# A third bank for the experts' first layer, one SSD block inside the last expert pass, and new instruction lists in a two-layer adaLN kernel

## Reference

```python
h = layernorm(x) * (1 + ca) + sa
x = x + ga * gated_delta_attention(h)      # q, k, v through silu, depthwise conv, silu; scan over 256 tokens of
                                           # S = a S - a b (S k) k' + b v k'; o = q S; then @ Wo.T
h = layernorm(x) * (1 + cb) + sb
x = x + gb * mixture(h)                    # router, top 2 of 8 experts; every expert is 128 -> 512 (silu) -> 128
h = layernorm(x) * (1 + ca2) + sa2
x = x + ga2 * ssd(h)                       # in-projection, causal conv, chunks of 64 tokens: cumsum, exp, two
                                           # first-order scans, state across chunks, normalisation, out-projection
h = layernorm(x) * (1 + cb2) + sb2
x = x + gb2 * ffn(h)                       # 128 -> 512, butterflies folded into the two matrices, gelu, 512 -> 128
```

## Time and profile before

| what | us |
| --- | --- |
| median of 3 runs | 489.74 |
| the runs | 491.87, 489.74, 486.61 |
| the profiled execution | 488.66 |
| its span in the trace | 486.8 |
| TensorE busy | 429.1 (88%) |
| ScalarE busy | 362.7 (74%) |
| VectorE busy | 346.9 (71%) |
| GpSimd busy | 162.7 (33%) |

### The profile page before, as it was taken

One profiled execution on the slowest core, in us unless ns is written; L12 is line 12 of the kernel. 1 busy time (PEld: TensorE's weight loads), 2 busy tenths in 40 slices (PEclk: granted clock), 3 DMA queues, 4 the chain that ended last, 5 costly groups with the idle time before them and its releaser, 6 DMA issues. The chain is left out here.

```text
span 486.8 us, 7163 instructions
## 1 busy us (share of the span) xinstructions
PE 429.1 (88%) x2164; PEld 312.5 (64%) x2164; DVE 346.9 (71%) x897; ACT 362.7 (74%) x629; POOL 162.7 (33%) x231
## 2 busy tenths in 40 slices
PE   4796987869897899999999999999999878999666
PEld 2675845548684776567667666767677556698434
DVE  3565998759899874999999899998325582222872
ACT  4889779587875759699669885869988889555324
POOL 1143840872359751267840272071100002000010
PEclk9789999799999799999999999999999999999899
DMA  7849892036600338000303811000001000000001
GB/s 199 288 127 267 286 309 80 0 85 173 159 2 0 88 99 213 19 0 1 87 1 85 208 39 23 1 1 0 2 0 24 0 1 1 22 1 1 0 1 23
DMA packets 34630, 35.49 MB, mean 73 GB/s; under 512 B 12824, under 2 KB 30752, under 8 KB 34336
## 3 DMA queue, kind: packets, MB, share of 16 engines
q1 hardware_dynamic: 34016, 30.57, 23.8%
q10 hardware_dynamic: 576, 4.46, 2.6%
HBM read 13.78 MB, written 1.05 MB: 30 GB/s over the span
## 5 line engine op out<-in xcount | busy, mean ns | idle before, releaser
L877 PEld LDWEIGHTS psS<-we2s,hid 128*128 128x128 f32 x1024 | 130.9, 195 | 36.6 <-issue 31.8
L862 PE MATMUL psF<-h,we1s 128*128 128x256 f32 (+1 forms) x384 | 136.8, 465 | 5.6 <-ACT hid L1645 4.8
L877 PE MATMUL psS<-we2s,hid 128*128 128x128 f32 x1024 | 133.4, 279 | 7.4 <-DVE acc L2319 6.6
L1645 ACT ACTIVATE hid<-psF,col 128x256 f32<-128x256 f32 (+1 forms) x192 | 99.6, 542 | 48.8 <-PE psF L862 44.4
L862 PEld LDWEIGHTS psF<-h,we1s 128*128 128x128 f32 x384 | 67.1, 195 | 38.4 <-issue 19.5
L3338 POOL TENSOR_TENSOR QS<-H,qn 128x256 f32<-128x256 f32 x64 | 55.1, 867 | 102.8 <-DVE H L2305 85.2
L2319 DVE SCALAR_TENSOR_TENSOR acc<-psS,gate,acc 128x128 f32<-128x128 f32 x128 | 41.0, 342 | 35.8 <-PE psS L877 35.7
L2305 DVE TENSOR_TENSOR_SCAN H<-A,psT 128x320 f32<-128x320 f32 x64 | 52.2, 816 | 1.3
L1447 ACT ACT_TABLE_LOAD x38 | 48.8, 1283 | 2.3 <-PEq L3646 1.7
L2277 DVE TENSOR_TENSOR psT<-wrep,H 128x360 f32<-128x360 f32 x63 | 40.2, 638 | 14.0 <-DMA wrep<-XX 12.5
L3389 POOL TENSOR_TENSOR x<-x,gdb 128x512 f32<-128x512 f32 (+1 forms) x5 | 4.6, 925 | 130.8 <-PE psM L691 129.4
(11 more groups left out here) (267 smaller groups left out, 650.1 us busy)
## 6 DMA issues: line engine op xcount, KB each, us to landing
wrep<-XX SPq DMA_DIRECT2D x72, 160.0 KB, 3.4
krep<-kn SPq DMA_DIRECT2D x64, 128.0 KB, 2.5
hid<-fold_mats_dram SPq DMA_DIRECT2D x22, 256.0 KB, 4.6
we1s<-we_dram ACTq DMA_DIRECT2D x1, 2048.0 KB, 10.8
we2s<-we_dram ACTq DMA_DIRECT2D x1, 2048.0 KB, 17.2
outT_dram<-x SPq DMA_DIRECT2D x3, 256.0 KB, 3.3
x<-xT_dram SPq DMA_DIRECT2D x2, 256.0 KB, 7.5
worep<-wo_rep_dram SPq DMA_DIRECT2D x1, 512.0 KB
```

The costliest lines, as they stand in the source:

```text
L862: mm(bank[name][:, 0:(b - a) * TWS[w]], we1s[:, e, k * P:(k + 1) * P], h2[w % 2][:, a * TWS[w]:b * TWS[w]], start=True, stop=True).then_in ...
L877: last = mm(bank[name][:, t * P:(t + 1) * P], hid[n % 2][:, k, t * P:(t + 1) * P], we2s[:, e, k, :], start=(k == 0), stop=(k == HT - 1))
L1645: nc.scalar.activation(hid[x_ % 2][:, k, 0:c], psF[n % 2][:, 0:c], ACT.Silu, bias=pc("be1", HT * e + k)).then_inc(s_hid_done, 1)
```

## The change

`LATE` is 4. In passes 4 and 5 the first layer takes turns on three banks, F0, F1 and T (`psT`, the recurrence's), and the first use of T waits until all 64 scans are done. Unit 3's SSD block, which came behind pass 5 from `ssd_steps` on, now lies inside pass 5, with `ssd_out(3)` just ahead of `experts_back(5)` on TensorE. `fill` can use other banks and half the width; there are eight fills in place of five. The lists of all engines are written anew; apart from the fills they hold the same items. The counts of table loads that follow from ScalarE's list are 68 before and 72 after; from the first `hidden(5, ...)` to the end 3 and 9. Units 0 to 2 and the windows 0 to 3 keep their computation; on SyncE, `spread_solved` now comes ahead of the next window's second `spread_keys`.

```diff
 SU = [(v, 0, NB) for v in range(NV - 1)] + [(NV - 1, 0, NB // 2), (NV - 1, NB // 2, NB)]
+LATE = len(EU) - 2
...
             return "F1" if u == LASTS[1] else "B"
 
+        def hid_bank(u, e, k):
+
+            n = HT * (EXPERTS * (u - LATE) + e) + k
...
             return G[j][:, 0:ncols(n) // CH, :]
 
...
-                name = f"F{n % 2}"
+                name = hid_bank(u, e, k)
+                if u == LATE and e == 0 and k == 2:
+                    pe.wait_ge(s_scan_done, SEQ // CH)
                 if e == 0 and k == 0:
...
-                free(f"F{i % 2}")
-                mm(psF[i % 2][:, :], cst("ident"), C[:, :, :].rearrange("p a n -> p (a n)"), start=True, stop=True)
+                name = ("B", "F0", "F1", "S0", "S1", "X0", "X1", "B")[i % 8]
+                parts = (4, 2)[i // 8 % 2]
+                free(name)
+                mm(bank[name][:, 0:parts * P], cst("ident"), C[:, 0:parts, :].rearrange("p a n -> p (a n)"), start=True, stop=True)
...
             variance(("front", 0))
             first_modulation()
             center(("front", 1))
-            for i in range(0, 5):
+            for i in range(0, 3):
                 project(0, i)
             variance(("front", 1))
+            project(0, 3)
+            fill(66)
+            project(0, 4)
             modulation()
...
             fold_down(7)
             fold_up(8)
+            fold_down(8)
             key_products(1, 0)
+            project(2, 0)
+            project(2, 1)
             key_products(1, 1)
-            for i in range(0, 4):
-                project(2, i)
+            project(2, 2)
+            project(2, 3)
             attn_out(0)
             project(2, 4)
             center(("moe", 0))
-            fill(59)
             variance(("moe", 0))
-            fold_down(8)
+            fill(87)
             center(("front", 3))
...
-            second(0, 0, 0)
-            first(0, 1, 2)
             second(0, 0, 1)
-            gate_rows(0)
-            first(0, 1, 3)
+            for i in range(1, 4):
+                first(0, 1, i)
             first(0, 2, 0)
             first(0, 2, 1)
+            gate_rows(0)
+            first(0, 2, 2)
             router_bias(0)
-            second(0, 1, 0)
-            first(0, 2, 2)
             first(0, 2, 3)
             variance(("front", 3))
             square_sums(2, 0)
             square_sums(2, 1)
+            first(0, 3, 0)
+            first(0, 3, 1)
+            second(0, 1, 0)
+            fill(133)
             second(0, 1, 1)
-            first(0, 3, 0)
+            first(0, 3, 2)
...
+            variance(("ssd", 2))
             second(4, 0, 0)
-            variance(("ssd", 2))
             second(4, 0, 1)
-            first(4, 2, 0)
-            second(4, 1, 0)
             first(4, 2, 1)
             first(4, 2, 2)
+            second(4, 1, 0)
+            fill(117)
             second(4, 1, 1)
-            first(4, 2, 3)
             ssd_steps(2)
             ssd_in(2)
...
+            experts_back(4)
+            for i in range(1, 4):
+                first(5, 2, i)
+            first(5, 3, 0)
+            center(("ssd", 3))
             second(5, 1, 0)
-            first(5, 2, 2)
-            first(5, 2, 3)
+            variance(("ssd", 3))
             second(5, 1, 1)
-            first(5, 3, 0)
+            second(5, 2, 0)
+            second(5, 2, 1)
             first(5, 3, 1)
-            second(5, 2, 0)
             first(5, 3, 2)
+            ssd_steps(3)
             first(5, 3, 3)
-            second(5, 2, 1)
-            first(5, 4, 0)
-            first(5, 4, 1)
+            for i in range(0, 4):
+                first(5, 4, i)
+            first(5, 5, 0)
+            ssd_in(3)
             second(5, 3, 0)
-            first(5, 4, 2)
-            first(5, 4, 3)
             second(5, 3, 1)
-            center(("ssd", 3))
-            first(5, 5, 0)
-            first(5, 5, 1)
             second(5, 4, 0)
-            first(5, 5, 2)
-            first(5, 5, 3)
+            for i in range(1, 4):
+                first(5, 5, i)
             second(5, 4, 1)
             first(5, 6, 0)
             first(5, 6, 1)
+            ssd_conv(3)
+            first(5, 6, 2)
             second(5, 5, 0)
-            first(5, 6, 2)
+            second(5, 5, 1)
             first(5, 6, 3)
-            second(5, 5, 1)
-            first(5, 7, 0)
-            first(5, 7, 1)
+            for i in range(0, 4):
+                first(5, 7, i)
             second(5, 6, 0)
-            variance(("ssd", 3))
-            first(5, 7, 2)
-            first(5, 7, 3)
             second(5, 6, 1)
             second(5, 7, 0)
             second(5, 7, 1)
+            ssd_out(3)
             experts_back(5)
-            ssd_steps(3)
             center(("ssd", 4))
-            ssd_in(3)
+            center(("ffn", 3))
             variance(("ssd", 4))
+            fill(130)
             ssd_steps(4)
-            ssd_conv(3)
             ssd_in(4)
+            variance(("ffn", 3))
             ssd_conv(4)
-            fill(51)
-            fill(55)
-            ssd_out(3)
-            fill(48)
-            center(("ffn", 3))
+            fill(80)
+            fill(132)
             ssd_out(4)
-            variance(("ffn", 3))
+            ffn_up(3, 0)
+            ffn_up(3, 1)
             center(("ffn", 4))
             variance(("ffn", 4))
-            ffn_up(3, 0)
-            fill(39)
-            for i in range(1, 4):
-                ffn_up(3, i)
+            fill(110)
+            ffn_up(3, 2)
+            ffn_up(3, 3)
             ffn_up(4, 0)
             ffn_up(4, 1)
             ffn_down(3)
...
             for i in range(0, 4):
                 hidden(5, 2, i)
+            ln_square(("ssd", 3))
+            ln_scale(("ssd", 3))
             for i in range(0, 4):
                 hidden(5, 3, i)
-            for i in range(0, 4):
-                hidden(5, 4, i)
-            for i in range(0, 4):
+            hidden(5, 4, 0)
+            hidden(5, 4, 1)
+            ssd_steps(3)
+            hidden(5, 4, 2)
+            hidden(5, 4, 3)
+            for i in range(0, 3):
                 hidden(5, 5, i)
+            ssd_in(3)
+            hidden(5, 5, 3)
+            ssd_decay(3)
+            ssd_gate(3)
+            ssd_shifted(3)
             for i in range(0, 4):
                 hidden(5, 6, i)
-            ln_square(("ssd", 3))
             for i in range(0, 4):
                 hidden(5, 7, i)
-            ln_scale(("ssd", 3))
-            ssd_steps(3)
+            ssd_norm(3)
             ln_square(("ssd", 4))
             ln_scale(("ssd", 4))
-            ssd_in(3)
+            ln_square(("ffn", 3))
             ssd_steps(4)
-            ssd_gate(3)
-            ssd_decay(3)
-            ssd_shifted(3)
+            ssd_in(4)
             ssd_gate(4)
-            ssd_in(4)
+            ssd_decay(4)
             ssd_shifted(4)
-            ssd_decay(4)
-            ssd_norm(3)
+            ln_scale(("ffn", 3))
             ssd_norm(4)
-            ln_square(("ffn", 3))
-            ln_scale(("ffn", 3))
+            ffn_act(3, 0)
+            ffn_act(3, 1)
             ln_square(("ffn", 4))
             ln_scale(("ffn", 4))
-            for i in range(0, 4):
-                ffn_act(3, i)
...
             chunk_delta(1, 3)
             chunk_outer(1, 3)
+            mix(0, 0, 0)
             chunk_scan(1, 3)
+            ln(("front", 3))
             chunk_seed(1, 4)
             chunk_delta(1, 4)
             chunk_outer(1, 4)
             chunk_scan(1, 4)
-            ln(("front", 3))
+            mix(0, 0, 1)
             chunk_seed(1, 5)
             chunk_delta(1, 5)
             chunk_outer(1, 5)
-            mix(0, 0, 0)
             chunk_scan(1, 5)
             chunk_seed(1, 6)
+            mix(0, 1, 0)
             chunk_delta(1, 6)
             chunk_outer(1, 6)
-            mix(0, 0, 1)
             chunk_scan(1, 6)
...
+            experts_residual(4)
             mix(5, 0, 1)
             mix(5, 1, 0)
             mix(5, 1, 1)
+            ln(("ssd", 3))
+            clear_last()
+            modulate(("ssd", 3))
+            ssd_sum(3)
             mix(5, 2, 0)
-            experts_residual(4)
             mix(5, 2, 1)
+            ssd_halo(3)
             mix(5, 3, 0)
+            ssd_least(3)
             mix(5, 3, 1)
+            ssd_steps(3)
+            ssd_gap(3)
+            ssd_most(3)
+            ssd_shift(3)
+            ssd_input(3)
             mix(5, 4, 0)
-            ssd_halo(3)
+            ssd_weights(3)
             mix(5, 4, 1)
             mix(5, 5, 0)
+            ssd_values(3)
+            ssd_norms(3)
             mix(5, 5, 1)
+            ssd_total(3)
+            ssd_norm(3)
             mix(5, 6, 0)
             mix(5, 6, 1)
             mix(5, 7, 0)
             mix(5, 7, 1)
-            ln(("ssd", 3))
-            modulate(("ssd", 3))
+            ssd_residual(3)
             experts_residual(5)
-            ssd_sum(3)
```

(89 more changed lines are left out.)

1036 lines of the change are left out of this document (520 added, 516 removed).

## The result

Median of four runs each: 489.12 us before (486.61 to 491.87), 476.63 after (475.77 to 477.89), ratio 0.9757 with a 95% interval of 0.972 to 0.9795. Two later comparisons gave 0.9811 (0.9759 to 0.9863) and 0.9773 (0.9747 to 0.9799). The forecast was 483.8, so the sign held, the time lay inside the range near its fast end, and the gain (12.5 us in the medians, 10.9 in the profiled pair) was about twice the 5.9 us of the sum. The profiled execution of after took 477.89 us, its span 475.9: 10.9 less than the span of 486.8.

A forecast was written before the change was run, and what follows sets the result against it. TensorE was taken as the bound from 167 to 375 us and in pass 5, with gains only elsewhere. From 488.66 us, -3.0 - 3.0 + 4.3 - 4.2 = -5.9 gave 482.8, with 1.08 for the median 483.8; range 475.5 to 495.

The forecast's parts named there:

- the cover of ScalarE's load blocks: In pass 5, TensorE's queued work was to hide ScalarE's two table-load blocks, all but about 1.2 and 0.5 us.
- (c): Pass 5 takes in unit 3: +2.6 us of matmuls and +1.7 of waits, +4.3 together; bounds +2.6 to +9.
- (d): What follows pass 5, from TensorE's last second to the end: 33.2 us for 37.4, so -4.2; bounds -8 to -1.
- (a): The lists up to 167 us: four early waits change, -3.0 us together; bounds -8 to +3.
- (b): Pass 4 with three banks: a third bank shortens tile runs and waits, -3.0 us; bounds -6 to +1.5.
- Waits of `first` for hid gone: Sign to look for in pass 4: first no longer waits for hid, and the pass is some 3 us shorter.
- 2.3 us of runs beyond their work: In pass 4, matmul runs longer than their work, part of about 5 us that a third bank can touch.
- The rival of ScalarE as the bound of pass 5: Pass 5: ScalarE's load blocks stop the hidden tiles and TensorE, nothing covered; +3.3 us, 493 us; chance 0.22.
- No change: Early waits move to the next item in the queue and pass 4 brings 2 us; 487.8 us; chance 0.18.
- The clock rival: Early stretches: fills and shorter waits keep TensorE's clock up, 6 us more gain, 477.8 us; chance 0.15.

The follow-up runs named there:

- e6: The changed kernel with second(5, 1, 1), second(5, 2, 0) and second(5, 2, 1) moved ahead of unit 3's variance; 480.37 us, 0.9814 of before.
- e7: The changed kernel with second(5, 6, 0) and second(5, 6, 1) moved ahead of first(5, 7, 1); 480.03 us, 0.9814 of before.
- e2: The changed kernel's new lists with two banks instead of three; 492.84 us, 1.0077 of before.
- e3: The new lists up to the start of pass 4, the lists of before behind it, two banks; 483.74 us, 0.9891 of before.
- e8: The changed kernel without its eight fills; 481.60 us, 0.9857 of before.
- e10: The changed kernel with VectorE's mix(0, 0, 0), mix(0, 0, 1) and mix(0, 1, 0) back at their places of before; 477.67 us, 0.9805 of before.
- e12: The changed kernel unaltered, run again as a measure for its variants; 478.52 us, 0.9811 of before.
- e15: The changed kernel without the four fills behind pass 5; 479.64 us, 0.9789 of before.
- e18: The changed kernel unaltered, run a third time as a measure; 477.94 us, 0.9773 of before.
- e9: The changed kernel with gate_rows(0) ahead of first(0, 1, 3) again, three tiles earlier; 481.29 us, 0.9878 of before.
- e1: The lists of before with the first layer of passes 4 and 5 on three banks; 491.59 us, 1.0056 of before.
- e5: The lists of before up to the first tiles of pass 5, the new ones behind, third bank from pass 5 on; 483.49 us, 0.9871 of before.

## Why the prediction was right or wrong

**The step that failed** is the cover of ScalarE's load blocks, in (c) and in (d). I let an expert's two `second`s of pass 5 count 0.89 us, the row of 8 records in the earlier trace rows, and that row is one `second` (one `second` is four accumulated steps, two records each). So in (c) TensorE had twice the second-layer work behind each block that I gave it, and the waits that I added there, 1.2 + 0.5 = 1.7 us, measured 0. In (d) I had ScalarE's `ssd_norm(3)` begin 0.9 us before TensorE's last step where it began 3.0 before (442.46, 445.50). The trace shows the covers whole and e6 and e7 show that these `second`s are what covers, with 1.9 and 2.0 us when they are taken away. This one step makes 1.7 us of the miss in (c) and 2.3 in (d), 4.0 of the 5.0 between the sum and the profiled pair.

- (a) -3.0: measured -5.1 in the profiled pair, and -3.8 as a mean over five traces of the old lists (365.7) and ten of the new (361.9: after, e2, e3, e6, e7, e8, which has no early fills, e10, e12, e15, e18). That the size came near is luck, for its make-up was wrong: the wait of `gate_rows(0)` went whole (2.50 us, not 1.3) and e9 bears this term out; the place of `mix(0, 0, 1)` gave nothing (e10); the wait of `second(1, 2, 0)` fell by 1.7 for my 1.5, untested; `project(3, 0)` waits 1.85 us less where I had 1.75 more. The 1.3 us beyond the means is the scatter of the start, described in the last section.
- (b) -3.0: measured -1.4. "Waits of `first` for hid gone" was wrong. I had read them as a matter of banks, and in after ScalarE's blocks fill three banks as well. What I had as the smaller part, 2.3 us of runs beyond their work, is the part that gave: 1.2 of the 1.4. The bank alone is +2.7 (e1), outside my bound of +1.5, and without it the new lists lose 15 us (e2).
- (c) +4.3: measured +2.6, my lower bound and exactly the matmuls put in (e5 gives 2.6 too). No wait at `ssd_steps(3)` or ahead of `first(5, 6, 3)`.
- (d) -4.2: measured -7.0. x was ready 2.3 us behind TensorE (445.50 to 447.81) and not 4.6; the chain to the norm took 12.7 for my 13.0, the rest 15.4 for 15.6. But I had the fills at nothing, and without them (e8, e15) the chain takes 12.7 or 13.4 and the rest 16.7 or 16.8. So the chain "alone" was sized rightly, and that the rest came out near my 15.6 is luck: its terms were some 1.2 us too fast, and the fills gave that back.
- Sum: -5.9 against -10.9; (a) short by 2.1, (c) by 1.7, (d) by 2.8, (b) long by 1.6.

The rival of ScalarE as the bound of pass 5 was refuted: it is busy for 23.26 of 30.90 us there and nobody waits for it. "No change" is refuted by (c) with (d) alone, 4.4 us. The clock rival named 477.8, near the measured time, but that is luck too: it was partly right, in another place than I had it. In the early stretches the granted clock went from 0.89, 0.85, 0.79 to 0.96, 0.92, 0.77, and e12 has 0.92 and 0.86 in the first two with the same code. Over the first 167 us it is 0.93 before and 0.94, 0.94 and 0.96 in after, e12 and e18; my estimate from 0.01 of 167 us is that it carries at most some 2 us of the 5.1 in the profiled pair, not 6. In the last stretch of all it is the fills that keep it near 1.00 (0.99 for 0.90, e8 and e15).

I called (c) with (d) "worth next to nothing"; it is 4.4 us, 40% of the gain. The other part is mostly the early lists.

## What to carry to other kernels

Before a block of work is priced as a stall, count how many records one item of the list leaves in the trace and add up the items queued behind the block; a factor of two in the cover made 4.4 us of gain look like nothing. A buffer more and the instruction order that uses it are one change, to be tried together: each alone was slower than before, by 0.6% and 0.8%. Where an engine's queue is full for most of what follows, an early delay arrives almost whole (11.4 us at the start of pass 1 were 10.9 at the end), so the early stretches deserve the same care as the chain that ends last.
